# Beginning the codes of fifteen tiles instead of twelve in the first pass over a 4096-node graph, and re-dealing the tiles and the expansions of the second pass

## What is computed

```python
def _ggc(x, adj, W, wih, whh, bih, bhh):          # 4096 nodes, 64 features
    m = adj @ (x @ W)
    gi, gh = m @ wih.T + bih, x @ whh.T + bhh      # split in r, z, n
    r, z = sigmoid(i_r + h_r), sigmoid(i_z + h_z)
    n = tanh(i_n + r * h_n)
    return (1.0 - z) * n + z * x
# layer 0: two gated steps with the same 4096 x 4096 adj, then residual and layernorm
x = layernorm(x + relu(ggc(relu(ggc(x, adj, ...)), adj, ...)))
# layer 1: every node keeps only its last 100 neighbours, each weighted by 2 ** -(number of kept edges behind it)
mask = (adj != 0); rank = cumsum(mask, axis=1); deg = rank[:, -1:]
k = minimum(deg, 100); pos = rank - (deg - k)
w = mask * where(pos > 0, 0.5 ** (k - pos), 0.0)
x = layernorm(x + w @ (x @ weight) + bias)
```

## Time and profile before

| | |
|---|---|
| median of 3 runs | 353.23 us (352.85 to 354.26) |
| profiled execution, its own time | 352.96 us |
| its span | 351.2 us |
| PE busy | 329.9 us (94%) |
| DVE busy | 302.4 us (86%) |
| ACT busy | 180.7 us (51%) |
| POOL busy | 24.8 us (7%) |
| PE's wait for x1s / for h_c in pass 2 | 2.0 us in 2 waits / 1.1 us in 2 waits |

### The profile page before, as it was taken

How to read it: one execution, slowest core, us unless ns; L and a number is a source line. 1 busy time by engine, 2 the same in 40 slices (tenths; PEclk the granted TensorE clock), 3 DMA queues, 4 the chain that set the end, 5 groups by cost and what they waited for, 6 DMA issues and landing times. The chain is left out here.

```text
span 351.2 us, 6769 instructions
## 1 busy us (share of the span) xinstructions
PE 329.9 (94%) x2536; PEld 154.2 (44%) x2536; DVE 302.4 (86%) x510; ACT 180.7 (51%) x235; POOL 24.8 (7%) x32
## 2 busy tenths in 40 slices
PE   1997999999999999999999999999999999979992
PEld 0441323233333333333333324444444454869992
DVE  0689879898999999997995667899899999888996
ACT  0202403114031140367467448977996969676993
POOL 2000000000000000000000001202020202022044
PEclk9999999999999999999999999999999999999999
DMA  7999999999999999999899999999999995000012
GB/s 243 413 411 410 410 407 409 409 409 397 405 361 331 392 377 363 365 318 342 294 359 316 376 411 406 406 350 326 358 380 370 383 383 215 17 1 4 2 32 91
DMA packets 32720, 111.10 MB, mean 316 GB/s; under 512 B 3632, under 2 KB 6192, under 8 KB 32688
## 3 DMA queue, kind: packets, MB, share of 16 engines
q1 hardware_dynamic: 31824, 109.20, 82.2%
q10 hardware_dynamic: 864, 1.48, 1.2%
HBM read 109.62 MB, written 1.05 MB: 315 GB/s over the span
## 5 line engine op out<-in xcount | busy, mean ns | idle before, releaser
L448 PE MATMUL m_acc<-stream,s_in 128*64 128x512 f32 x512 | 126.7, 603 | 4.0 <-DMA stream<-in_adj_t 3.1
L911 DVE TENSOR_SCALAR codes<-stream 128x1024 uint8<-128x1024 f32 x117 | 77.1, 686 | 6.6 <-DMA stream<-in_adj_t 6.3
L448 PE MATMUL out<-stream,s_mid 128*64 128x512 f32 x272 | 68.5, 593 | 0.2 <-DMA stream<-in_adj_t 0.2
L448 PEld LDWEIGHTS m_acc<-stream,s_in 128*64 128x64 f32 x512 | 34.4, 138 | 70.9 <-issue 47.9
L448 PE MATMUL m_acc<-stream,s_mid 128*64 128x512 f32 x240 | 55.2, 599 | 0.1
L851 POOL TENSOR_TENSOR rstd<-var,mhalf 128x4 f32<-128x4 f32 x16 | 23.0, 1436 | 322.7 <-DVE var L1066 322.7
L960 DVE SCALAR_TENSOR_TENSOR codes<-codes,run 128x384 uint32<-128x384 uint32 (+2 forms) x56 | 43.0, 768 | 1.9
L955 DVE TENSOR_TENSOR run<-run,codes 128x768 uint16<-128x768 uint16 (+2 forms) x55 | 41.5, 755 | 1.8
L646 ACT ACTIVATE m_high<-m_acc 64x512 f32<-64x512 f32 x13 | 7.7, 596 | 58.0 <-PE m_acc L448 45.1
L448 PEld LDWEIGHTS out<-stream,s_mid 128*64 128x64 f32 x272 | 19.5, 137 | 38.1 <-issue 37.4
L678 ACT ACTIVATE rz<-gate_ps,b_rz 128x256 f32<-128x256 f32 x32 | 13.4, 469 | 43.7 <-PE gate_ps L516 43.6
(11 more groups left out here) (139 smaller groups left out, 375.2 us busy)
## 6 DMA issues: line engine op xcount, KB each, us to landing
stream<-in_adj_t SPq DMA_DIRECT2D x204, 512.0 KB, 6.4
x_res<-in_x_pairs SPq DMA_DIRECT2D x8, 128.0 KB, 6.8
out_nodes<-stream SPq DMA_DIRECT2D x8, 128.0 KB, 2.1
hx<-in_x_pairs ACTq DMA_DIRECT2D x1, 512.0 KB, 7.5
const<-in_consts ACTq DMA_DIRECT2D x1, 358.0 KB, 6.7
hx<-in_x_pairs ACTq DMA_DIRECT2D x2, 128.0 KB, 6.1
hx<-in_x_pairs ACTq DMA_DIRECT2D x1, 256.0 KB, 8.8
bias_b<-in_bias SPq DMA_DIRECT2D x1, 128.0 KB, 5.4
```

Source lines behind the costliest of these rows:

```text
L448: last = nc.tensor.matmul(to[D * u:D * (u + 1), :], state[:, t * D:(t + 1) * D], stream[:, n % SLOTS, u * CW:(u + 1) * CW], start=start[u] ...
L911: nc.vector.tensor_scalar(edges(p // 2, b, 2 * (p % 2), 2), stream[:, n % SLOTS, :], 0.0, None, ALU.not_equal).then_inc(mask_made, 1)
```

## The change

N_EARLY becomes 15: parts 0 and 1 of tiles (3, 3), (3, 2) and (3, 1) are done in pass 1, three in chunk 5 and three in chunk 7, and part 2 of them in pass 2. In chunk 5 three masks go from DVE to ACT. In pass 2 CHAIN deals 6, 7, 5, 4, 4, 4, 2, 0, 0 tiles to stages 0 to 8, where it was 5, 5, 5, 4, 4, 4, 4, 1, 0. Expansions of three blocks, (0, 5), (4, 4) and (3, 5), go from ACT to DVE and that of (5, 3) from DVE to ACT. The stages at which expansions are placed change from stage 3 on, in stages 6 to 8 and the end loop most.

```diff
-CHAIN_EARLY = ({3: (11, 13, 15), 4: (4, 7, 10, 13), 5: (4, 7, 10, 14), 6: (4,)},
-               {6: (10, 11, 12, 13, 14, 14), 7: (2, 4, 6, 8, 10, 12)})
+CHAIN_EARLY = ({3: (11, 13, 15), 4: (4, 7, 10, 13), 5: (3, 5, 7, 9, 11, 13, 15), 6: (4,)},
+               {6: (10, 11, 12, 13, 14, 14), 7: (2, 3, 5, 6, 7, 8, 9, 10, 12)})
...
-BY_SIGN = {6: (8, 9, 11, 13, 14), 7: (1, 8, 9, 11, 13, 14)}
+BY_SIGN = {5: (8, 11, 13), 6: (8, 9, 11, 13, 14), 7: (1, 8, 9, 11, 13, 14)}
...
-BY_DVE = [AHEAD[4], AHEAD[6]] + [REST[n] for n in (2, 3, 5, 7, 9, 11, 12, 14, 16, 18, 19, 21, 22, 24, 26, 28, 30, 32,
-                                         34)]
+BY_DVE = [AHEAD[2], AHEAD[4], AHEAD[6], AHEAD[7], AHEAD[8]] + \
+    [REST[n] for n in (2, 5, 7, 9, 11, 12, 14, 16, 18, 19, 21, 22, 24, 26, 28, 30, 32, 34)]
...
-    [(4, 3), REST[0], REST[1], AHEAD[7], AHEAD[8]] + \
+    [(4, 3), REST[0], REST[1]] + \
...
-ACT_EXPANDS = {1: (1, 1, 1), 2: (1, 2, 2), 3: (1, 2, 3), 4: (1, 2, 2), 5: (1, 2, 2),
-               6: (1, 2, 2), 7: (1, 1, 1), 8: (1, 1, 3)}
-DVE_EXPANDS = {1: (0, 0, 0), 2: (0, 0, 0), 3: (0, 0, 0), 4: (0, 0, 1), 5: (0, 0, 1), 6: (0, 0, 1),
-               7: (1, 0, 2), 8: (2, 1, 4)}
-ACT_END = (2, 1, 1, 1, 1, 0, 0, 0)
-DVE_END = (2, 2, 1, 1, 1, 1, 0, 0)
+ACT_EXPANDS = {1: (1, 1, 1), 2: (1, 2, 2), 3: (1, 2, 2), 4: (1, 2, 2), 5: (1, 2, 2),
+               6: (1, 2, 2), 7: (0, 1, 2), 8: (0, 1, 4)}
+DVE_EXPANDS = {1: (0, 0, 0), 2: (0, 0, 0), 3: (0, 0, 1), 4: (0, 0, 1), 5: (0, 0, 1), 6: (1, 1, 1),
+               7: (0, 1, 1), 8: (1, 1, 6)}
+ACT_END = (1, 1, 1, 1, 1, 0, 0, 0)
+DVE_END = (2, 1, 1, 1, 1, 1, 0, 0)
...
-CHAIN = [chain_tiles(*x) for x in ((0, 5), (5, 10), (10, 15), (15, 19), (19, 23), (23, 27), (27, 31),
-                                   (31, 32), (32, 32))]
-CHAIN_CUT = [(1, 2), (2, 4), (2, 3)] + [(1, 2)] * 4 + [(0, 1)] * 2
+CHAIN = [chain_tiles(*x) for x in ((0, 6), (6, 13), (13, 18), (18, 22), (22, 26), (26, 30), (30, 32),
+                                   (32, 32), (32, 32))]
+CHAIN_CUT = [(1, 2), (3, 5), (2, 3)] + [(1, 2)] * 3 + [(0, 1)] * 3
```

## The result

The changed kernel takes 356.58 us (median of six runs, 354.88 to 356.8), the kernel before 353.43 us in the same series (352.7 to 354.26): a ratio of 1.0079, 95% interval 1.0061 to 1.0097. That is +3.15 us, where +2.4 was forecast. The profiled execution took 356.55 us by its own time, with a span of 354.8 us.

A forecast was written before the change was run, and what follows sets the result against it. PE bounds the kernel, busy from about 80 to 300 us; its pass 2 waits make 3.07 us. Terms 0.98 + 0.75 + 0.9 - 0.4 + 0.2 = +2.4 us gave 355.7 us; forecast 355.0 to 356.6 (chance 0.60), range 354.0 to 357.2.

The forecast's parts named there:

- Pass 1: Chunks 5 and 7: more DVE work, second sum some 0.9 us late, third on time; 0 for PE, bound 3.3 us.
- Stage 0: Six small tiles, not five, stand ahead of combine(8), so gates(8) starts 0.98 us later, with nothing to cover it.
- Stage 1: Three tiles, not two, ahead of sum_squares delay x1s and gates(9): +0.75 us, 1.73 so far.
- Stages 2 and 3: Tile (3, 0) with its maximum delays n_input(10): waits of 0.35 us at node(10), 0.55 at block (1, 3); +0.9.
- Stage 7: Counted from gates(14), G: node(14)'s wait goes, x1s at G + 10.0, gates(15) at G + 10.85; gives 1.9 us.
- Stage 8's start: Two ACT expansions ahead of sigmoids(15): node(15) at 18.25 us behind gates(14), waiting 2.2 us; takes most of 1.9 back.
- Stages 7 and 8: From gates(14) to node(15): 18.25 us where it was 18.64, together -0.4 us.
- Rival 1: The two expansions don't hold sigmoids(15), or the lag in stages 2 and 3 is swallowed: 353.3 to 355.0 us; chance 0.24.
- The end: Behind node(15): DVE reaches the end loop 1.3 us later and makes up all but 0.2; +0.2 us (0 to 0.4).
- The clock: TensorE's clock behind its waits: kept at full by the profile row of the 1.64 us wait, so nothing was added.
- Rival 4: Clock falls behind the wait at node(15): four blocks at double time, +3.6 us, about 359 us; chance 0.03.
- The rule cited in the prediction: Skill page: the array's clock is halved after idling, so a wait can cost more than its length; not priced in.

The follow-up runs named there:

- Experiment 4: Kernel before with only the pass 1 part: fifteen tiles begun, three masks of chunk 5 on ACT; 353.1 us, ratio 1.0006.
- experiment 5: Changed kernel with five tiles in stage 0 and eight in stage 1, so tiles ahead of combine(8) and x1s(1) are as before; 356.07 us, ratio 1.0092.
- experiment 8: Kernel before, twelve tiles begun, with expansions newly placed: none between split_high(7) and sigmoids(15), none ahead of square(7); 350.54 us, ratio 0.9936.

## Why the prediction was right, and what it left out

The forecast of 355.7 us is 0.9 us under the measured 356.58. The direction came as forecast, and so did the places and sizes of the waits; the clock's part did not. The terms are counted from S. The second profile of the changed kernel stands for it, since its S (199.87 us) is that of before (199.83).

- **Pass 1, forecast 0.** Experiment 4 bounds it at 0.7 us. In the changed kernel's first profile DVE runs through to the second sum at 187.06 without the 2.43 us of idle time in the earlier trace rows, and reaches the third at 189.98. With S 0.48 us sooner that is 1.2 us late (0.9 forecast) and then on time. PE shows no wait for it.
- **Stage 0, forecast +0.98.** gates(8) stands 6.47 us behind S (205.82 - 199.35), before 5.48: +0.99.
- **Stage 1, forecast 1.73 in all.** gates(9) stands 18.00 us behind S (217.35 - 199.35), before 16.34: +1.66.
- **Stages 2 and 3, forecast +0.9.** Waits of 0.27 and 0.53 us, where 0.35 and 0.55 were forecast. In the second profile gates(14) stands at 300.16, 100.29 behind S, before 97.88: +2.41 in all, 0.2 less than the forecast 2.63. But the wait at x1s and the wait at mx are no property of the sixth tile, as the prediction's working suggests: with that tile back in its place the same loss showed up at node(9), at block (0, 3) and at node(10) (experiment 5).
- **Stage 7, forecast gates(15) at G + 10.85.** It came at 311.06 - 300.25 = G + 10.81, and x1s at G + 9.97 (forecast 10.0).
- **Stage 8's start, forecast node(15) at G + 18.25 and a wait of 2.2 us.** It came at G + 18.20 with 2.04 us. Stages 7 and 8 gave -0.44 (forecast -0.4). Rival 1 needed node(15) at G + 16.05.
- **The end, forecast +0.2.** Where the clock held, the rest behind node(15) took 36.85 us, before 36.61: +0.24. Where it fell, this term can't be told apart from the 1.25.
- **The clock, forecast 0.** This is the missing term, and the step that failed reads "By the row the sum stays +2.4". The row was a wait of 1.64 us. The last row ends at 310 us, ahead of that wait, and doesn't show the clock behind it. These windows of the same trace do, at 1.00:

```profile
310.00:315.00 5.00, 4.51 (x68) 3.68 (x69) 4.75 (x9) 3.63 (x6) 0.00 (x0) 1.00 0.01 2
315.00:320.00 5.00, 4.50 (x78) 4.20 (x76) 4.90 (x8) 4.09 (x3) 0.82 (x1) 1.00 0.01 3
```

I carried that over to a wait of 2.04 us, a quarter longer than any that the trace of before could vouch for, and a single profile vouches for little: the wait of 2.04 us itself left the clock at 1.00 in three profiles of seven, and one of 1.69 us brought it down in experiment 8. Rival 4 had the mechanism and the place, with a chance of 0.03, and its price of 3.6 us was almost three times the measured 1.25: the lower clock covered only part of the four blocks, and the end loop gave a little back.

The sum without the clock is 2.41 - 0.44 + 0.24 = +2.2 us (forecast 2.4). With it, +3.5 us. So the terms of the sum were right to within 0.2 us each, and that the median still lies within the forecast's 355.0 to 356.6 us, by 0.02, is partly luck: the clock stood at 0 in that band, and its room was meant for the other terms. In the first profile a pair was also late once: PE waited 0.4 us for a load at 268 us, and gates(14) stands 0.6 us later behind S than in the other three profiles of the changed kernel, which show no such wait. That was not forecast.

The rule cited in the prediction bore on this case after all. The Trainium skill, page "TensorE: Matmul & The Clock Gate", section "What's actually happening", lets the clock drop after idle time, and it adds that the hardware's looks at activity run on their own and don't start with the kernel. The trace agrees with the first: 4 of 7 executions with the same wait lost the clock. With the second it is compatible and no more: the fall came once during node(15) and otherwise behind it. On how much idle time it takes, page and traces differ, and the traces decide: 2.04 us was enough in these four, and 1.69 us in experiment 8.

**Still open:** that one wait brings the clock down in some executions and not in others fits looks that fall at other times each run, but no run here shows those looks, so this cause is only argued. Whether the waits of 1.64 us (before) and 1.63 us (experiment 4) at gates(15) cost no clock by their length, by their place or by chance is open too: it is one profile each, 1.69 us was enough elsewhere, and no run made that wait longer by itself. Nor does any run tell the length of one wait from how busy PE was around it.

## What to carry to other kernels

Where a forecast moves two waits of a matmul engine into one, price the one wait by its length and by the clock behind it, and give the clock a real chance as soon as the wait is near or above the longest that the trace shows at full clock, for one profile at 1.00 doesn't make a wait harmless; splitting the wait over two or three places kept 1.1 to 1.6 us here with the late engine just as late. In a queue that runs in order, ask of each long optional instruction (here a 2 us expansion on ACT) which due instruction stands right behind it: moving one of them by one place was worth 2.6 to 2.9 us (1.5 of it the wait, the rest mostly the clock), nearly as much as the whole change cost, 3.15 us. And when a wait is to be cured by moving the instruction ahead of it, first see whether the engine's load up to the next wait falls, or whether the wait only moves.

## What the hardware showed that I had not expected

- A wait of 2.04 us of TensorE, with PE busy for 2.96 of the 5 us around it, took the granted clock to 0.66 to 0.69 from 320 to 325 us in three profiles; in a fourth it stood at 0.83 in both stretches, and in three it stayed at 1.00 (0.97 to 1.00 in the stretch of the wait itself). A wait of 1.69 us in pass 1 took it to 0.51 over 2 us, once. The loss behind the 2.04 us is 1.62 us on the four blocks (5.37 against 3.75) and 1.25 us on the kernel.
- The clock was back at 1.00 in the very next 5 us, with PE busy throughout.
- The same program's start of pass 2 moves by up to half a microsecond from one execution to the next (S at 199.35 to 199.87 in four profiles of the changed kernel), which blurs a loss of 1.25 us that comes and goes in a list of run times; counted from node(15) on it stands out to 0.05 us.
